# Causal mask of the row maxima moved from TensorE's matmuls into one fused VectorE instruction, with the stage's loops written out

## The chip, the cores and the metric

The kernel runs on one core of a Trainium2 chip. TensorE, VectorE, ScalarE and GpSimd work beside each other and meet at semaphores; SyncE issues the DMAs. The metric is the device time of one launch in microseconds: 903.62 us as the median of three runs (902.7 to 904.41). The times of the profile come from one further execution.

## The reference

Four layers run one after another over an input of 8 batches x 512 tokens x 128 features: dilated attention with a ternary feed-forward, a gated attention, a causal attention with grouped heads, and a mixture of experts. The change concerns the third:

```python
q = (x @ wq.T).reshape(B, S, 16, 8)
k = (x @ wk.T).reshape(B, S, 4, 8)      # repeated for 16 heads
v = (x @ wv.T).reshape(B, S, 4, 8)
attn = jnp.einsum('bqhd,bkhd->bhqk', q, k) / sqrt(8)
attn = jnp.where(causal, attn, -inf)
attn = jax.nn.softmax(attn, axis=-1)
out = jnp.einsum('bhqk,bkhd->bqhd', attn, v)
```

B is 8, S is 512, with 16 heads. A softmax is computed with the maximum of each row taken off first, so every head needs the 512 maxima of its causal rows.

## The kernel before, in words

The causal attention is a stage of its own (`causal_attention_phase`, names beginning with `d_`). The stage ahead of it (`projection_phase`, names `c_`) computes the queries and keys, splits each into bf16 parts that add up to the fp32 value, and SyncE stores them in DRAM (`q_stack`, `k_stack`) by batch. Its end waits for all these stores, and then for all engines. The causal stage loads the stacks back as 96 rows (`Qs`, `Ks`), one pair of buffers for even and one for odd batches.

A batch is worked on twice. In the *first* pass (function `first` on TensorE, `maxima` on VectorE) TensorE multiplies queries with keys, tokens of the query along the partitions, into two PSUM banks `pS` that alternate. A head has three *fills* of a bank: 512 keys for the last 128 queries (f = 0), 384 keys (f = 1), and 256 + 128 keys for the first two blocks of queries (f = 2). Behind each product a second matmul of an identity with a 128x128 triangle of -1e30 (`top.mask_bf`) adds the causal mask to its last 128 columns. VectorE reduces each block to a maximum per row (`mx`). A fill starts when VectorE is through with the fill two before it (semaphore `S_max`), and VectorE starts on a fill when TensorE has ended it (semaphore `S`). When a batch has all its maxima, `split` cuts them into three bf16 parts, TensorE turns them (`rows`), and a trip through DRAM makes them six more rows beside the stacks.

In the *second* pass (`second`) TensorE multiplies keys with queries, this time with the maxima taken off, into `pT`; ScalarE takes the exponential into `P`; GpSimd zeroes the triangle there (`affine_select`, L1167); TensorE multiplies with the values (`values`, into `pO`); ScalarE copies `pO` out, TensorE turns it (`by_token`, into `pM`), and VectorE divides by the sums (`divide`).

The order is written out by hand. A step (one batch) has 8 pairs of heads of 3 units. TensorE does in a unit: the second pass for this unit, two fills of the first pass of a later batch, and, by a pattern of period six units (`turn`), one of four value products, or the turning of an output, or neither. VectorE does the same two fills' maxima and, once in six units, a `divide`. The fills run three pairs (`LEAD`) ahead of the batch: the last three pairs of step n fill heads of batch n + 2. Ahead of the first step, all of batch 0 and six heads of batch 1 are filled with nothing beside them.

Step 0 and step 7 are written out; steps 1 to 6 are a hardware loop of three rounds of two steps (`Fori` in `steps`), so waits in it compare with counts held in registers. Since each round is the same code, step 6 too loads and fills a batch n + 2 = 8, which does not exist: `q_stack` and `k_stack` have a ninth entry, into which the projection stage stores the last batch a second time (`(0, 1, 1)` in its SyncE block), and the first pass of six heads is run on it. Nobody uses these maxima.

Of the kernel before, what the change touches and what calls it, by code (L numbers as in the profile page):

```python
# [35 lines left out]


def wait_alone(eng, sem, count, unit=1):


    if not isinstance(count, int):
        count = eng.to_reg(count)
        eng.wait_ge(sem, unit)
    eng.wait_ge(sem, count)
# [749 lines left out]
def projection_phase(nc, top, dram):  # L794

    with ExitStack() as ctx:
# [217 lines left out]
def causal_attention_phase(nc, top, dram):  # L1014
# [11 lines left out]
    with ExitStack() as ctx:  # L1026
        ph = Phase(nc, ctx, "d_")
        sm = ph.sems("zeros ones ones_from max_ones S S_max part1 rest1 part2 rest2 parts mT_psum mT ST P masked PV O_sb O_T rden O_tok")
# [15 lines left out]
        rden = ph.sb("rden", [128, QT, 2, 2])  # L1044
        pS = [ph.ps(f"pS{k}", [128, 512]) for k in two]
# [11 lines left out]
        def wait(eng, sem, value):  # L1057

            if not isinstance(value, int) or value > 0:
                eng.wait_ge(sem, value)  # L1060

        def steps(eng, step):
# [15 lines left out]

        def turn(pair, unit, at):
# [5 lines left out]
        def turns(n, pair, unit, at):  # L1085

            got = turn(pair, unit, at)
            ended = isinstance(n, int) and n == B
            if got is None or (got[0] == 0 and ended) or (got[0] == 1 and isinstance(n, int) and n == 0):
                return []  # L1090
# [5 lines left out]
        parity = [0]  # L1096

        def par(n):

            if isinstance(n, int):  # L1100
                parity[0] = n % 2
            else:
                parity[0] = 1 - parity[0]
            return parity[0]

        with nc.Block() as block:

            @block.sync
            def _(sp):
# [22 lines left out]
                def step(n, m, more):  # L1132
                    c = par(n)
                    if more:
# [3 lines left out]
                        if not (isinstance(n, int) and n + 2 > B):  # L1138
# [4 lines left out]
                        sp.wait_ge(sm["ST"], n * NT + NT)  # L1143
                        load_stack(n + 2, c, 1)
# [7 lines left out]
                steps(sp, step)  # L1152

                for a in two:
                    sp.wait_ge(stacks[0][a], 64 * (B // 2 + 1))

            @block.gpsimd
            def _(pool):
                def step(n, m, more):
                    par(n)  # L1160
                    for pair in range(HEADS // 2):
                        for unit in range(3):

                            wait_alone(pool, sm["P"], n * NT + 3 * pair + unit + 1)
# [22 lines left out]
                steps(pool, step)  # L1187

            @block.vector
            def _(dve):  # L1190
                def maxima(n, c, some):
                    for k, f in some:
                        h, fill = ORDER[k], 3 * k + f
                        dve.wait_ge(sm["S"], n * NS + fill + 1)
                        src = pS[fill % 2]
                        if f < 2:
                            last = nc.vector.reduce_max(mx[c][:, 3 - f, h:h + 1], src[:, 0:512 - 128 * f], AX.X)  # L1197
                        else:
                            nc.vector.reduce_max(mx[c][:, 1, h:h + 1], src[:, 0:256], AX.X)  # L1199
                            last = nc.vector.reduce_max(mx[c][:, 0, h:h + 1], src[:, 256:384], AX.X)  # L1200
# [32 lines left out]
                def step(n, m, more):  # L1233
                    c = par(n)
                    for pair in range(HEADS // 2):
                        if more and pair == SPLIT_AT:
                            split(n + 1, 1 - c)
                        for unit in range(3):
                            if more:
                                for ahead, k, f in fills(pair)[2 * unit:2 * unit + 2]:  # L1240
# [8 lines left out]
                steps(dve, step)  # L1249
# [5 lines left out]
            def _(act):  # L1255
# [11 lines left out]
                def step(n, m, more):  # L1267
                    c = par(n)
# [16 lines left out]
                steps(act, step)  # L1285
# [5 lines left out]
            def _(pe):  # L1291
# [3 lines left out]
                def first(n, m, c, some):  # L1295

                    for k, f in some:
# [60 lines left out]
                def rows(n, c):  # L1358

                    if not (isinstance(n, int) and n == 0):  # L1360
                        wait_alone(pe, sm["O_tok"], (n - 1) * NG + 1)
                    wait_alone(pe, sm["parts"], n + 1)
# [5 lines left out]
                def step(n, m, more):  # L1368
                    c = par(n)
                    for pair in range(HEADS // 2):  # L1370
                        for unit in range(3):
                            second(n, m, c, pair, unit)
                            if more:
                                for ahead, k, f in fills(pair)[2 * unit:2 * unit + 2]:
# [8 lines left out]
                steps(pe, step)  # L1383
# [410 lines left out]
```

## Time and profile before

| | |
|---|---|
| launch, median of 3 runs | 903.62 us |
| span of the profiled execution | 900.7 us (no time of its own is given beyond the span; the median stands 2.9 us above it) |
| TensorE busy | 643.0 us (71%) |
| VectorE busy | 559.2 us (62%) |
| ScalarE busy | 403.3 us (45%) |
| GpSimd busy | 222.6 us (25%) |
| maxima L1197, L1199, L1200 | 160.9 + 56.3 + 37.6 us in 268 + 134 + 134 instructions |
| mask matmuls | 111.4 us in 536 instructions |
| GpSimd's triangle in `P`, L1167 | 101.0 us in 256 instructions |
| the page's first group of products of the first pass, all four shapes | 150.4 us in 536 instructions |

The causal stage runs from its first loads at 402 us to 754 us. A busy time sums what the records cover; matmuls overlap one another, so TensorE's is more than it needs. What one instruction costs its engine is the distance from its start to the next start where neither waits. "Idle before" names whom an engine waited for.

### The profile page before, as it was taken

Reading aid. Unit: us, or ns where it says so; the run is one execution under the profiler, and the core shown is the slowest. Engines: PE = TensorE matmul, PEld = TensorE weight load, DVE = VectorE, ACT = ScalarE, POOL = GpSimd, SP = SyncE. Lnnn points to the kernel's source line nnn. Section 1 sums busy time; section 2 is a strip of 40 time slices with the busy share of each in tenths; the row PEclk is TensorE's granted clock in tenths of the full one; section 3 lists DMA queues with packets and bytes.
Section 4 is the critical chain, followed back from the end, with each engine's and each line's share of the span. In section 5 each row is a group of like instructions: output and inputs, shape, how many; then the busy total and the mean of one; then the engine's idle time right before and its main releaser. Section 6 shows DMA issues by size and latency. Waiting matters only on the chain. (4 is left out here: it accounts for less than half of the span.)

```text
span 900.7 us, 13426 instructions
## 1 busy us (share of the span) xinstructions
PE 643.0 (71%) x4232; PEld 372.4 (41%) x4232; DVE 559.2 (62%) x1764; ACT 403.3 (45%) x794; POOL 222.6 (25%) x340
## 2 busy tenths in 40 slices
PE   0816338938754480708899999999999996789651
PEld 0816328117644270403244445454444523555320
DVE  5786974042463535307878878788787801478897
ACT  3682565410203424400046566665665673456541
POOL 1040310010003032333023333333333341134344
PEclk9957655555965665755579999999999997799896
DMA  6000000000000050253001111111011100000001
GB/s 236 1 0 1 1 1 1 0 2 1 1 1 0 1 175 0 70 168 81 17 1 49 36 37 30 33 40 42 26 38 33 36 13 1 0 1 1 23 24 47
DMA packets 19369, 28.61 MB, mean 32 GB/s; under 512 B 3310, under 2 KB 15102, under 8 KB 19146
## 3 DMA queue, kind: packets, MB, share of 16 engines
q1 hardware_dynamic: 18746, 25.94, 9.5%
q10 hardware_dynamic: 576, 2.10, 0.6%
q8 instruction: 23, 0.38, 0.2%
q14 instruction: 24, 0.20, 0.1%
HBM read 14.57 MB, written 11.35 MB: 29 GB/s over the span
## 5 line engine op out<-in xcount | busy, mean ns | idle before, releaser
L1276 ACT ACTIVATE d_P<-d_pT 128x768 f32<-128x768 f32 (+1 forms) x192 | 167.9, 881 | 110.8 <-PE d_pT L1293 110.8
L1197 DVE TENSOR_REDUCE d_mx<-d_pS 128x1 f32<-128x512 f32 (+1 forms) x268 | 160.9, 620 | 66.2 <-PE d_pS L1293 61.5
L1293 PE MATMUL d_pS<-d_Ks,d_Qs 96*128 96x512 bf16 (+3 forms) x536 | 150.4, 329 | 31.2 <-DMA d_Ks<-k_stack 25.1
L1167 POOL TENSOR_SCALAR_AFFINE_SELECT d_P<-d_P 128x256 f32<-128x256 f32 x256 | 101.0, 406 | 233.5 <-ACT d_P L1276 233.4
L1293 PE MATMUL d_pS<-mask_bf,ident_bf 128*128 128x128 bf16 x536 | 111.4, 236 | 0.0
L1293 PE MATMUL d_pT<-d_Qs,d_Ks 102*128 102x512 bf16 (+3 forms) x512 | 103.7, 305 | 1.1 <-ACT d_P L1276 0.5
L1293 PE MATMUL d_pO<-d_P,d_V 128*32 128x512 f32 (+3 forms) x1024 | 96.5, 451 | 1.9 <-POOL d_P L1167 1.5
L1293 PEld LDWEIGHTS d_pS<-d_Ks,d_Qs 96*128 96x128 bf16 x536 | 54.2, 101 | 100.1 <-DVE d_mx L1197 32.8
L1623 PE MATMUL e_PE<-gate_expT,e_oT 128*128 128x512 f32 x128 | 62.5, 634 | 11.0 <-DVE e_T L1519 10.4
L421 PE MATMUL a_PS<-ident,N 128*128 128x128 f32 x96 | 21.5, 403 | 63.5 <-ACT N L320 51.6
L1199 DVE TENSOR_REDUCE d_mx<-d_pS 128x1 f32<-128x256 f32 x134 | 56.3, 420 | 13.5 <-PE d_pS L1293 11.1
L1293 PEld LDWEIGHTS d_pT<-d_Qs,d_Ks 102*128 102x128 bf16 x512 | 35.7, 99 | 69.1 <-ACT d_P L1276 49.5
L1450 POOL TENSOR_TENSOR e_T<-e_T 128x512 f32<-128x512 f32 x32 | 40.7, 1279 | 93.5 <-DVE e_T L1519 77.9
L1293 PEld LDWEIGHTS d_pS<-mask_bf,ident_bf 128*128 128x128 bf16 x536 | 55.5, 104 | 7.1 <-issue 0.3
L1605 ACT ACTIVATE e_T<-e_PE,e_comb 128x128 f32<-128x128 f32 x128 | 34.7, 383 | 45.0 <-PE e_PE L1623 19.6
L421 PEld LDWEIGHTS a_PS<-ident,N 128*128 128x128 f32 x96 | 17.8, 212 | 66.7 <-ACT N L320 54.6
L415 POOL TENSOR_TENSOR X<-X,a_nT 128x1024 f32<-128x1024 f32 x8 | 19.5, 2433 | 92.0 <-ACT a_nT L320 92.0
L1623 PEld LDWEIGHTS e_PE<-gate_expT,e_oT 128*128 128x128 f32 x128 | 24.7, 205 | 40.8 <-issue 23.3
L990 PE MATMUL c_PA<-ident,c_a 128*128 128x128 f32 x32 | 7.9, 428 | 46.6 <-ACT c_a L950 46.6
L320 ACT ACTIVATE N<-X,a_nb,a_rs 128x128 f32<-128x128 f32 x96 | 37.8, 479 | 1.1 <-DVE a_nb L161 0.8
L1200 DVE TENSOR_REDUCE d_mx<-d_pS 128x1 f32<-128x128 f32 x134 | 37.6, 281 | 0.0
L1258 ACT ACTIVATE d_mT<-d_pM 48x512 bf16<-48x512 bf16 x8 | 4.7, 590 | 65.3 <-PE d_pM L1364 65.2
(256 smaller groups left out, 1056.8 us busy)
## 6 DMA issues: line engine op xcount, KB each, us to landing
d_Qs<-q_stack SPq DMA_DIRECT2D x36, 192.0 KB, 2.9
q_stack<-c_Qp SPq DMA_DIRECT2D x9, 384.0 KB, 2.7
q_stack<-c_Qp SPq DMA_DIRECT2D x9, 256.0 KB, 3.0
X<-in_x_dram ACTq DMA_DIRECT2D x4, 512.0 KB, 7.7
d_V<-V SPq DMA_DIRECT2D x8, 256.0 KB, 2.3
out_dram<-e_moe SPq DMA_DIRECT2D x4, 512.0 KB, 2.6
d_Ks<-k_stack SPq DMA_DIRECT2D x36, 48.0 KB, 2.8
w_qkvT<-in_w_qkvT_dram SPq DMA_DIRECT2D x1, 1536.0 KB
```

What stands on the lines that cost most here:

```text
L320: last = nc.scalar.activation(dst(t), src(t), ACT.Identity, bias=nb[c][:, t:t + 1], scale=rs[c][:, t:t + 1])
L415: nc.gpsimd.tensor_tensor(X[c][:, :, :], X[c][:, :, :], y[c][:, :, :], ALU.add).then_inc(sm[s + "_x"], 1)
L421: last = nc.tensor.transpose(dst(t), src(t), ident)
L1167: last = nc.gpsimd.affine_select(out=view, in_=view, compare_op=ALU.is_ge, fill=0.0, base=0, pattern=[[0, 2], [1, 128]], channel_multiplie ...
L1197: last = nc.vector.reduce_max(mx[c][:, 3 - f, h:h + 1], src[:, 0:512 - 128 * f], AX.X)
L1199: nc.vector.reduce_max(mx[c][:, 1, h:h + 1], src[:, 0:256], AX.X)
L1200: last = nc.vector.reduce_max(mx[c][:, 0, h:h + 1], src[:, 256:384], AX.X)
L1276: nc.scalar.activation(P[pair % 4][:, :, P_AT[unit]:P_AT[unit] + w], pT[(3 * pair + unit) % 2][:, :, 0:w], ACT.Exp, scale=float(HD4) ** -0 ...
L1293: return nc.tensor.matmul(out, lhsT, rhs, start=start, stop=stop)
L1450: nc.gpsimd.tensor_tensor(T[u % 4][:, 0:NE // 2, :], T[u % 4][:, 0:NE // 2, :], T[u % 4][:, NE // 2:NE, :], ALU.add).then_inc(sm["halved"], 1)
L1605: last = nc.scalar.activation(T[u % 4][:, e, :], PE_[1][:, e, :], ACT.Copy, scale=comb[u // CT][:, u % CT, e:e + 1])
L1623: return nc.tensor.matmul(out_, lhsT, rhs, start=start, stop=stop)
```

## The change

VectorE's `tensor_tensor_reduce` takes the product from PSUM and a mask from SBUF, adds them, writes the sum (bf16, to `masked_S`, read by nobody) and gives the maximum of each row. The mask `wide_mask` is 384 columns of zero and then the triangle; each block reads its last w columns, and it is built once by a memset and a copy with one wait. The mask matmuls go. The loop is replaced by eight written-out steps, so all waits compare with constants (`wait_alone` goes), and nothing is stored, loaded or filled for a ninth batch (`fills_of`, `n + 2 < B`).

```diff
-                    for b in (0, 1, 1) if k == CHUNKS - 1 else (0, 1):
-                        entry = 2 * k + b + (1 if n_stored[c] == 12 * (k // 2) + 12 else 0)
+                    for b in two:
+                        entry = 2 * k + b
...
+        wide_mask = ph.sb("wide_mask", [128, 512], BF16)
+        masked_S = [ph.sb(f"masked_S{k}", [128, 512], BF16) for k in two]
...
-            step(0, 0, True)
-            with eng.Fori(0, B // 2 - 1) as i:
-                step(2 * i + 1, i, True)
-                step(2 * i + 2, i + 1, True)
-            step(B - 1, B // 2 - 1, False)
+            for n in range(B):
+                step(n, n // 2, n % 2, n < B - 1)
...
+        def fills_of(n, pair, unit):
+
+            return [(ahead, k, f) for ahead, k, f in fills(pair)[2 * unit:2 * unit + 2] if n + ahead < B]
...
-                        sp.wait_ge(sm["ST"], n * NT + NT)
-                        load_stack(n + 2, c, 1)
+                        if n + 2 < B:
+                            sp.wait_ge(sm["ST"], n * NT + NT)
+                            load_stack(n + 2, c, 1)
...
-                        if f < 2:
-                            last = nc.vector.reduce_max(mx[c][:, 3 - f, h:h + 1], src[:, 0:512 - 128 * f], AX.X)
-                        else:
-                            nc.vector.reduce_max(mx[c][:, 1, h:h + 1], src[:, 0:256], AX.X)
-                            last = nc.vector.reduce_max(mx[c][:, 0, h:h + 1], src[:, 256:384], AX.X)
+                        for q, at in ((3, 0),) if f == 0 else ((2, 0),) if f == 1 else ((1, 0), (0, 256)):
+                            w = 128 * q + 128
+                            last = nc.vector.tensor_tensor_reduce(
+                                out=out_[:, at:at + w], in0=src[:, at:at + w], in1=wide_mask[:, 512 - w:512],
+                                scale=1.0, scalar=LOWEST, op0=ALU.add, op1=ALU.max,
+                                accum_out=mx[c][:, q, h:h + 1])
...
+                nc.vector.memset(wide_mask[:, 0:384], 0.0)
+                nc.vector.tensor_copy(wide_mask[:, 384:512], top.mask_bf[:, :]).then_inc(sm["mask_wide"], 1)
+                dve.wait_ge(sm["mask_wide"], 1)
...
-                            mm(dst[:, at:at + w], Qs[c][0:ALL_ROWS, i, 128 * q:128 * q + 128],
-                               Ks[c][0:ALL_ROWS, h // 4, 0:w], True, False)
-                            last = mm(dst[:, at + w - 128:at + w], top.ident_bf[:, :], top.mask_bf[:, :],
-                                      False, True)
+                            last = mm(dst[:, at:at + w], Qs[c][0:ALL_ROWS, i, 128 * q:128 * q + 128],
+                                      Ks[c][0:ALL_ROWS, h // 4, 0:w])
```

On TensorE, in step 0 behind the turning of the maxima of batch 0, one unit and the start of the next stand like this before (`d_pT` is the second pass, `d_pS` a fill):

```order
L1293 MATMUL d_pT<-d_Qs,d_Ks 128x384 x2
L1293 MATMUL d_pS<-d_Ks,d_Qs 128x256
L1293 MATMUL d_pS<-mask_bf,ident_bf 128x128
L1293 MATMUL d_pS<-d_Ks,d_Qs 128x128
L1293 MATMUL d_pS<-mask_bf,ident_bf 128x128
L1293 MATMUL d_pS<-d_Ks,d_Qs 128x512
L1293 MATMUL d_pS<-mask_bf,ident_bf 128x128
L1293 MATMUL d_pT<-d_Qs,d_Ks 128x256
```

The same place in the changed kernel:

```order
L1274 MATMUL d_pT<-d_Qs,d_Ks 128x384 x2
L1274 MATMUL d_pS<-d_Ks,d_Qs 128x256
L1274 MATMUL d_pS<-d_Ks,d_Qs 128x128
L1274 MATMUL d_pS<-d_Ks,d_Qs 128x512
L1274 MATMUL d_pT<-d_Qs,d_Ks 128x256
```

Four matmuls a head go, each behind its product; nothing else is in another place.

On VectorE, at the first head of the stage (before, L1197 twice, for f = 0 and f = 1) and what follows it:

```order
L1197 TENSOR_REDUCE d_mx<-d_pS 128x1 x2
L1199 TENSOR_REDUCE d_mx<-d_pS 128x1
L1200 TENSOR_REDUCE d_mx<-d_pS 128x1
```

And now, from the building of the mask on:

```order
L1225 MEMSET d_wide_mask 128x192
L1226 COPY d_wide_mask<-mask_bf 128x128
L1177 ISA d_masked_S,d_mx<-d_pS,d_wide_mask 128x512
L1177 ISA d_mx 128x1
L1177 ISA d_masked_S,d_mx<-d_pS,d_wide_mask 128x384
L1177 ISA d_mx 128x1
L1177 ISA d_masked_S,d_mx<-d_pS,d_wide_mask 128x256
L1177 ISA d_mx 128x1
L1177 ISA d_masked_S,d_mx<-d_pS,d_wide_mask 128x128
L1177 ISA d_mx 128x1
```

Each of the four reductions of a head has become two instructions: the fused one and one that writes the row's maximum out of the engine's accumulator.

On SyncE, at the end of the projection stage, before (the last six are the second copy of the last batch):

```order
L832 DMA q_stack<-c_Qp 128x3x512
L834 DMA k_stack<-c_Kp 32x3x512
L832 DMA q_stack<-c_Qp 128x2x512
L834 DMA k_stack<-c_Kp 32x2x512
L832 DMA q_stack<-c_Qp 128x512
L834 DMA k_stack<-c_Kp 32x512
L819 UNCONDITIONAL_BRANCH
L1108 UNCONDITIONAL_BRANCH
L1114 DMA d_Qs<-q_stack 48x2048
```

And now, where these rows are the only copy:

```order
L823 DMA q_stack<-c_Qp 128x3x512
L825 DMA k_stack<-c_Kp 32x3x512
L823 DMA q_stack<-c_Qp 128x2x512
L825 DMA k_stack<-c_Kp 32x2x512
L823 DMA q_stack<-c_Qp 128x512
L825 DMA k_stack<-c_Kp 32x512
L810 UNCONDITIONAL_BRANCH
L1091 UNCONDITIONAL_BRANCH
L1097 DMA d_Qs<-q_stack 48x2048
```

The branch and the first load of the causal stage have moved up by six DMAs.

## Rows read from the trace of the kernel before

**Rows 1.** The page, part 2: granted TensorE clock in 40 slices of 22.5 us

```profile
PEclk9957655555965665755579999999999997799896
```

**Rows 2.** Timeline, TensorE, one period: start us, us, engine, line, operation, tiles

```profile
541.05 0.49 PE L1293 MATMUL d_pT<-d_Qs,d_Ks 102*128 102x384 bf16 x2
...
543.03 0.50 PE L1293 MATMUL d_pT<-d_Qs,d_Ks 102*128 102x256 bf16 x4
...
543.54 0.22 PE L1293 MATMUL d_pS<-mask_bf,ident_bf 128*128 128x128 bf16 x1
...
543.60 0.27 PE L1293 MATMUL d_pS<-d_Ks,d_Qs 96*128 96x256 bf16 x1
...
544.76 0.61 PE L1293 MATMUL d_pT<-d_Qs,d_Ks 102*128 102x512 bf16 x2
...
546.37 0.50 PE L1293 MATMUL d_pT<-d_Qs,d_Ks 102*128 102x384 bf16 x2
...
547.72 0.50 PE L1293 MATMUL d_pT<-d_Qs,d_Ks 102*128 102x256 bf16 x4
...
548.76 0.59 PE L1293 MATMUL d_pT<-d_Qs,d_Ks 102*128 102x512 bf16 x2
...
550.32 0.49 PE L1293 MATMUL d_pT<-d_Qs,d_Ks 102*128 102x384 bf16 x2
```

**Rows 3.** Timeline, VectorE, where it does not wait

```profile
540.40 1.16 DVE L1197 TENSOR_REDUCE d_mx<-d_pS 128x1 f32<-128x512 f32 x2
...
541.48 0.25 DVE L1222 RECIPROCAL d_rden<-d_pM 128x16 f32<-128x16 f32 x1
...
542.14 0.41 DVE L1199 TENSOR_REDUCE d_mx<-d_pS 128x1 f32<-128x256 f32 x1
```

**Rows 4.** Groups of VectorE (a two-part instruction), then timeline of ScalarE's accumulator reads

```profile
L1480 DVE MATCH_VALUE_LOAD e_index<-e_best,e_logit 128x8 f32 x32 | 2.3, 73 | 0.0
...
762.91 0.19 ACT L1581 ACTIVATION_READ_ACCUMULATOR e_moe<-e_h 128x1 f32 x1
763.00 0.29 ACT L1581 ACTIVATE e_moe<-e_h 128x128 f32<-128x128 f32 x1
```

**Rows 5.** Timeline of the experts stage, VectorE beside GpSimd

```profile
807.82 1.27 POOL L1450 TENSOR_TENSOR e_T<-e_T 128x512 f32<-128x512 f32 x1 [3.62 <-DVE e_T L1519]
808.60 1.22 DVE L1460 TENSOR_TENSOR e_h<-e_PA,N 128x1024 f32<-128x1024 f32 x1
...
831.74 2.34 POOL L1445 TENSOR_TENSOR e_moe<-e_h,X 128x1024 f32<-128x1024 f32 x1
831.84 2.26 DVE L1501 TENSOR_TENSOR e_w<-e_w 128x8 f32<-128x8 f32 x1
```

**Rows 6.** Timeline, SyncE's last stores and TensorE's first fill

```profile
390.88 0.44 SPq L832 DMA_DIRECT2D q_stack<-c_Qp  x1
...
393.76 0.44 SPq L834 DMA_DIRECT2D k_stack<-c_Kp  x1
...
406.78 0.61 PE L1293 MATMUL d_pS<-d_Ks,d_Qs 96*128 96x512 bf16 x1 [25.09 <-DMA d_Ks<-k_stack]
```

**Rows 7.** Timeline, TensorE in the last step, which has no fills

```profile
720.30 1.07 PE L1293 MATMUL d_pO<-d_P,d_V 128*32 128x512 f32 x8
...
727.10 1.06 PE L1293 MATMUL d_pO<-d_P,d_V 128*32 128x512 f32 x8 [0.38 <-issue]
```

**Rows 8.** Timeline, ScalarE, the same instruction of three steps

```profile
519.68 0.59 ACT L1258 ACTIVATE d_mT<-d_pM 48x512 bf16<-48x512 bf16 x1
...
557.28 0.59 ACT L1258 ACTIVATE d_mT<-d_pM 48x512 bf16<-48x512 bf16 x1 [0.31 <-PE d_pM L1364]
...
595.26 0.59 ACT L1258 ACTIVATE d_mT<-d_pM 48x512 bf16<-48x512 bf16 x1 [0.30 <-PE d_pM L1364]
```

**Rows 9.** Timeline, VectorE ahead of the first step, heads 1 and 16 of batch 0

```profile
409.03 0.42 DVE L1199 TENSOR_REDUCE d_mx<-d_pS 128x1 f32<-128x256 f32 x1 [0.34 <-PE d_pS L1293]
...
440.49 0.42 DVE L1199 TENSOR_REDUCE d_mx<-d_pS 128x1 f32<-128x256 f32 x1
```

More of the change, by code:

```diff
@@ L35 @@
 NEG = -8.0
[L38 to L44, printed above, removed]
 class Phase:
@@ L1027, in causal_attention_phase @@
         ph = Phase(nc, ctx, "d_")
-        sm = ph.sems("zeros ones ones_from max_ones S S_max part1 rest1 part2 rest2 parts mT_psum mT ST P masked PV O_sb O_T rden O_tok")
+        sm = ph.sems("mask_wide zeros ones ones_from max_ones S S_max part1 rest1 part2 rest2 parts mT_psum mT ST P masked PV O_sb O_T rden O_tok")
         two = range(2)
@@ L1057, in wait, with steps @@
         def wait(eng, sem, value):
-            if not isinstance(value, int) or value > 0:
+            if value > 0:
                 eng.wait_ge(sem, value)
-        def steps(eng, step):
-            step(0, 0, True)
-            with eng.Fori(0, B // 2 - 1) as i:
-                step(2 * i + 1, i, True)
-                step(2 * i + 2, i + 1, True)
-            step(B - 1, B // 2 - 1, False)
+        def steps(step):
+            for n in range(B):
+                step(n, n // 2, n % 2, n < B - 1)
         def fills(pair):
@@ L1087, in turns @@
             got = turn(pair, unit, at)
-            ended = isinstance(n, int) and n == B
-            if got is None or (got[0] == 0 and ended) or (got[0] == 1 and isinstance(n, int) and n == 0):
+            if got is None or (got[0] == 0 and n == B) or (got[0] == 1 and n == 0):
                 return []
@@ L1130, in max_rows, with step @@
                             .then_inc(rows_in[c], 16)
-                def step(n, m, more):
-                    c = par(n)
+                def step(n, m, c, more):
                     if more:
@@ L1151, in _, with step @@
                 max_rows(0, 0, 0)
-                steps(sp, step)
-                for a in two:
-                    sp.wait_ge(stacks[0][a], 64 * (B // 2 + 1))
+                steps(step)
             @block.gpsimd
             def _(pool):
-                def step(n, m, more):
-                    par(n)
+                def step(n, m, c, more):
                     for pair in range(HEADS // 2):
                         for unit in range(3):
-                            wait_alone(pool, sm["P"], n * NT + 3 * pair + unit + 1)
+                            pool.wait_ge(sm["P"], n * NT + 3 * pair + unit + 1)
                             for at in ((P_AT[0],), (P_AT[1],), P_AT[2:])[unit]:
@@ L1186, in _ @@
                             .then_inc(sm["max_ones"], 1)
-                steps(pool, step)
+                steps(step)
             @block.vector
@@ L1231, in divide, with step @@
                     last.then_inc(sm["O_tok"], 1)
-                def step(n, m, more):
-                    c = par(n)
+                def step(n, m, c, more):
                     for pair in range(HEADS // 2):
@@ L1239, in step @@
                             if more:
-                                for ahead, k, f in fills(pair)[2 * unit:2 * unit + 2]:
+                                for ahead, k, f in fills_of(n, pair, unit):
                                     b, _, b_c = others(n, m, c, ahead)
@@ L1248, in _ @@
                 maxima(1, 1, everything[:6 * LEAD])
-                steps(dve, step)
+                steps(step)
                 for pair, unit in LAST_TURNS:
@@ L1284, in _ @@
                 rows(0, 0)
-                steps(act, step)
+                steps(step)
                 for pair, unit in LAST_TURNS:
@@ L1358, in rows @@
                 def rows(n, c):
-                    if not (isinstance(n, int) and n == 0):
-                        wait_alone(pe, sm["O_tok"], (n - 1) * NG + 1)
-                    wait_alone(pe, sm["parts"], n + 1)
+                    wait(pe, sm["O_tok"], (n - 1) * NG + 1)
+                    pe.wait_ge(sm["parts"], n + 1)
                     for q in range(QT):
@@ L1366, in rows, with step @@
                     last.then_inc(sm["mT_psum"], 1)
[L1368 to L1369 removed]
+                def step(n, m, c, more):
                     for pair in range(HEADS // 2):
@@ L1373, in step @@
                             if more:
-                                for ahead, k, f in fills(pair)[2 * unit:2 * unit + 2]:
+                                for ahead, k, f in fills_of(n, pair, unit):
                                     first(*others(n, m, c, ahead), [(k, f)])
@@ L1382, in _ @@
                 first(1, 0, 1, everything[:6 * LEAD])
-                steps(pe, step)
+                steps(step)
                 for pair, unit in LAST_TURNS:
```

18 lines of the change are left out of this document (5 added, 13 removed).

## The prediction, made before the changed kernel had run

> **What bounds the kernel now.** I read the shares of the engines first: TensorE 71%, VectorE 62%, so neither is idle enough to be ignored nor full enough to be the bound alone. The chain of waits begins only at 754 us, behind the causal stage, because all engines meet there. So the stage is in series with the rest, and what it saves the kernel saves. The change touches this stage and the end of the one before it. TensorE's clock is at its low level (1.2 GHz) in slices 18 and 19, ahead of the first step, and at its high level (2.4 GHz) from slice 21 to 32, which takes in steps 1 to 6 and the first part of step 7 [rows 1].
>
> Then the timeline of one period, which is two pairs or four heads. Its six units start on TensorE at 541.05, 543.03, 544.76, 546.37, 547.72 and 548.76, and the next period at 550.32 [rows 2]: 1.98, 1.73, 1.61, 1.35, 1.04 and 1.56 us, 9.27 in all. The first four hold the value products and are long; the fifth holds none, the sixth the turning of an output.
>
> VectorE's price of a maximum is its start-to-start distance where it does not wait. A 512 and a 384 block took from 540.40 to 541.48, 1.08 us [rows 3]. A reduction of 256 columns is recorded with 0.41 us and an addition of 1024 with 1.22 [rows 3, 5]: 0.81 us for 768 columns, 1.04 to 1.06 ns each, and I take 1.042. The 896 columns are then 0.933 of the 1.08 us, so an instruction costs its columns + 0.073 us. The three fills of a head cost 0.606 (f = 0), 0.473 (f = 1) and 0.267 + 0.133 + 0.146 = 0.546 us. A divide takes from 541.48 to 542.14, 0.66 us [rows 3]. By unit, with the fills in their order (1, 1.15; 2, 1.02; 3, 1.08; 4, 1.15; 5, 1.02; 6, 1.08 + 0.66 = 1.74), VectorE needs 7.16 us in a period.
>
> The two banks let one engine run ahead by about a unit at most. I therefore take, for each unit, the longer of the two engines: 1.98, 1.73, 1.61, 1.35, 1.04, 1.74, sum 9.45. The trace has 9.27, so this rule is 2% too long, and I use it for differences only.
>
> **The change part by part.**
>
> *The stores.* The second copy of the last batch is issued from 390.88 to 393.76 + 0.44 = 394.20 us, 3.3 us, and nothing computes there: TensorE's first fill waited 25.09 us for a DMA [rows 6]. The causal stage begins when the stores have landed, so the whole 3.3 us goes: **-3.3**. It could be 2.8 to 3.8, since a store's landing and not its issue ends the wait.
>
> *Six heads of no use.* Step 6's last three pairs lose their fills. A period without fills is 727.10 - 720.30 = 6.80 us [rows 7] against 9.27, so three pairs save 1.5 x 2.47 = **-3.7**. The turning of batch 7's maxima in that step could come 0.5 us late for want of cover.
>
> *The loop.* From 519.68 to 557.28 both steps are of one round, 37.60 us; from 557.28 to 595.26 a round ends between them, 37.98 us [rows 8]. So a round's end costs 0.38 us, and there are an entry, two returns and an exit: between 0.8 (returns alone) and 1.5 us, **-1.0**. What the waits on registers cost is not seen apart; in the first units TensorE's matmuls stand close behind one another, so I take 0, and a gain from them would come on top.
>
> *Mask matmuls.* From 543.54 to 543.60 one is worth 0.06 us of TensorE at the high clock [rows 2]. 16 of them leave a period: 3, 3, 2, 3, 3, 2 by unit. TensorE's units become 1.80, 1.55, 1.49, 1.17, 0.86, 1.44.
>
> *The fused instruction.* It reads a product in PSUM and bf16 in SBUF. The nearest row is an addition of such a pair over 1024 columns, 1.22 us [rows 5], that is 1.067 for the columns and 0.15 that its neighbours partly cover; the reductions have the same 0.15. So I take the main part at the price of the reduction it replaces.
>
> *The accumulator read,* a second instruction with each, 16 in a period. The trace has none on VectorE. From below: the load half of a two-part instruction is recorded with 73 ns, and costs somewhat less from start to start, so 0.055 us. From above: ScalarE's accumulator read is recorded with 0.19 us [rows 4], if the engine may do nothing beside it; but on ScalarE the next instruction started 0.09 us after the read (762.91 to 763.00) [rows 4]. I take 0.073 us, what any small instruction costs here beyond its columns, and keep 0.055 and 0.19. VectorE's units become 1.15 + 0.22, 1.02 + 0.22, 1.08 + 0.15, 1.15 + 0.22, 1.02 + 0.22, 1.74 + 0.15 = 1.37, 1.24, 1.23, 1.37, 1.24, 1.89. The longer of the two: 1.80, 1.55, 1.49, 1.37, 1.24, 1.89, sum 9.34. Against 9.45 that is -0.11 a period. 106 heads are filled inside steps, 26.5 periods: **-2.9**. What the units with value products win, the others give back. Each further 10 ns of a read costs 0.08 a period (8 of the 16 reads lie in units that VectorE sets), 2.1 us in all.
>
> *The edge of a batch.* A step of 37.60 us is four periods of 9.27 and 0.52 for the split and the turning of the maxima. With VectorE later than before, less of the split is covered; I add the same again for six steps, rounded down: **+2.5** (0 to 4).
>
> *Ahead of the first step.* Head 1 to head 16 took 440.49 - 409.03 = 31.46 us, 2.10 a head [rows 9], where VectorE alone needs 1.63. The rest is the round trip of a bank at the low clock. The read lengthens that trip by what the missing mask matmul (0.11 us at this clock) shortens it: **0**, for 22 heads. Building the wide mask lies in the 25 us in which VectorE waits for the stacks. Loads of batch 8 that go were beside other work.
>
> Sum: -3.3 - 3.7 - 1.0 - 2.9 + 2.5 = -8.4 us, from the profiled span 900.7 to 892.3. The median stands 2.9 us above that span, so **895.2 us**.
>
> One rule of the skill speaks to the read. The microarchitecture page (Trainium skill, "Vector Engine (DVE) Microarchitecture Reference", section 5.2, Measured stream behaviour on trn2) gives 1.0417 ns a column and about 75 ns an instruction after overlap, the same for programs of several micro-ops. Taken for the read this is an estimate of 0.076 us, and the sum would stand within 1 us of the one above; no row here shows it for an accumulator.
>
> **The rivals.**
>
> *The accumulator read is not overlapped (slower).* If VectorE is held until the main part has ended and the read has been written, a read costs 0.19 us. VectorE's units become 1.72, 1.59, 1.46, 1.72, 1.59, 2.12, the longer ones 1.80, 1.59, 1.49, 1.72, 1.59, 2.12 = 10.31, +0.86 a period, +22.8 us; ahead of the first step a head takes 1.63 + 0.76 = 2.39 instead of 2.10, +6.4 us. With -8.0 for stores, heads and loop and +4 for the edges: +25, **929 us**. It tips at a read of about 0.105 us. For it: no row has this instruction, and its value goes to the engine's buffer release, as S_max now hangs on it. Against: ScalarE's pair overlaps.
>
> *VectorE and GpSimd block each other (slower).* The maxima now read SBUF, and GpSimd works a third of the period (256 instructions of 0.4 us in 32 periods: 3.2 us in each). An instruction of 8 columns took 2.26 us beside GpSimd's of 2.34, both of its inputs in SBUF [rows 5]. If a fused maximum that starts in such a time waits a quarter of a us, a third of 16 gives +1.3 a period on VectorE, 0.7 after overlap: +18, **914 us**. Against: an addition with one input in PSUM took 1.22 us though GpSimd's instruction covered its first 0.5 us [rows 5].
>
> This is what the Trainium skill says ("SBUF — State Buffer", Who interferes with whom): two SBUF inputs contend with GpSimd's reads, one does not. By that rule the rival costs nothing here, and the trace agrees with 1.22 against 2.26 us.
>
> *The reads are nearly free (faster).* At 0.03 to 0.055 us a read, with the split covered: -2.9 - 5 and no +2.5, **888 us**. The rows of a loading half with 73 ns speak for it a little.
>
> *TensorE's clock falls.* Its stage loses 16 short matmuls a period, but step 7 without any fill stays at the high level in slice 32 [rows 1]. In a step at 1.2 GHz a period would be some 4 us longer; 26.5 of them, 1000 us. I give it 2%.
>
> **How the numbers follow.** Forecast (read 0.06 to 0.09 us) 0.60: 890 to 901. Nearly free reads 0.12. A read of 0.09 to 0.12, with which the gain vanishes, 0.11: 900 to 907. Not overlapped 0.10; blocked by GpSimd 0.05; clock 0.02. A measurement of this kernel tells 0.2%, 1.8 us, from no change. Faster takes the forecast, the free reads and a little of the third, 0.74; same 0.07; slower the rest, 0.19. Leaving out most of the last three and the lowest tail, the range is 885 to 912.
>
> **What would show it.** The fused instruction's mean at 512 columns should be 0.69 us and the next start 0.61 + 0.07 later; a period from 541 on, read at the second pass's 512-column unit, 9.1 to 9.2 us; the stage's first fill 3.3 us earlier, near 403.5; no fills after pair 4 of step 6, and 3.7 us less there; VectorE busy near 90% in the steps, its waits for `d_pS` shrunk and TensorE's waits for `d_mx` grown. I am wrong if the read's start-to-start is over 0.1 us, if the fused part has a second cycle a column, or if TensorE's clock drops between 460 and 740 us.

## The result, and the profile after

The changed kernel took 875.68 us (median of 4, 875.22 to 875.80) against 903.16 (4 runs, 896.22 to 904.41): ratio 0.970, with a 95% interval of 0.966 to 0.974. The forecast was 895.2, range 885 to 912. The direction was right, the gain was 27.5 us instead of 8.4. The profiled execution took 875.76 us and spans 874.0 us (the one before spans 900.7).

Of several versions single executions (of e6 and e11 two each) reach the causal stage 12 to 15 us earlier than the others, so below stages are compared by their length (first fill of the causal stage to first matmul `e_PA` of the next) beside the medians.

The page of the kernel after, parts 1 and 2 (busy us, share, instructions; granted clock in 40 slices of 21.9 us):

```profile
PE 611.4 (70%) x3672; PEld 336.9 (39%) x3672; DVE 553.2 (63%) x2254; ACT 402.2 (46%) x794; POOL 222.5 (25%) x340
...
PEclk9967655555966575565569999999999996899896
```

TensorE lost 31.6 us of work. VectorE's busy time is no larger (559.2 before), though it executes 490 more instructions (512 reads came, 24 reductions of the ninth batch went): the reads' records lie beside others. The clock stays high through the steps, as before [rows 1], and in both kernels it falls for 3.4 us in the last value products, which the account below needs.

Groups of VectorE after, shapes apart, from 370 us on (count, busy us, mean ns, idle before them):

```profile
L1177 DVE CUSTOM_DVE_ANT_0 d_masked_S<-d_pS,d_wide_mask 128x512 bf16<-128x512 f32 x128 | 88.2, 689 | 22.3 <-PE d_pS L1274 22.2
L1177 DVE CUSTOM_DVE_ANT_0 d_masked_S<-d_pS,d_wide_mask 128x384 bf16<-128x384 f32 x128 | 71.1, 555 | 14.2 <-PE d_pS L1274 13.5
L1177 DVE CUSTOM_DVE_ANT_0 d_masked_S<-d_pS,d_wide_mask 128x256 bf16<-128x256 f32 x128 | 53.9, 421 | 5.2 <-PE d_pS L1274 2.4
L1177 DVE DVE_READ_ACCUMULATOR2_ANT d_mx<- 128x1 f32 x512 | 42.5, 83 | 0.0
L1177 DVE CUSTOM_DVE_ANT_0 d_masked_S<-d_pS,d_wide_mask 128x128 bf16<-128x128 f32 x128 | 36.6, 286 | 0.0
```

The fused instruction's 689 ns at 512 columns are the forecast's 0.69. Its means would be far above this if GpSimd held it up. So the main part was priced rightly; what of the read's 83 ns? The timeline of VectorE (start, us):

```profile
527.12 0.08 DVE L1177 DVE_READ_ACCUMULATOR2_ANT d_mx<- 128x1 f32 x1
527.12 0.42 DVE L1177 CUSTOM_DVE_ANT_0 d_masked_S<-d_pS,d_wide_mask 128x256 bf16<-128x256 f32 x1
527.47 0.08 DVE L1177 DVE_READ_ACCUMULATOR2_ANT d_mx<- 128x1 f32 x1
527.47 0.28 DVE L1177 CUSTOM_DVE_ANT_0 d_masked_S<-d_pS,d_wide_mask 128x128 bf16<-128x128 f32 x1
...
527.69 0.69 DVE L1177 CUSTOM_DVE_ANT_0 d_masked_S<-d_pS,d_wide_mask 128x512 bf16<-128x512 f32 x1
528.31 0.08 DVE L1177 DVE_READ_ACCUMULATOR2_ANT d_mx<- 128x1 f32 x1
528.31 0.55 DVE L1177 CUSTOM_DVE_ANT_0 d_masked_S<-d_pS,d_wide_mask 128x384 bf16<-128x384 f32 x1
528.79 0.08 DVE L1177 DVE_READ_ACCUMULATOR2_ANT d_mx<- 128x1 f32 x1
```

A fused instruction and its read start 0.62 us apart for 512 columns (527.69 to 528.31) and 0.48 for 384, which is the price of the plain reduction in the forecast (0.606 and 0.473) plus 0.01. The next fused instruction starts within 0.01 us of the read. The read lies in the last 0.08 us of the long record ahead of it, in which the next long one starts too. Over five batches (second to seventh `d_mT`), where nothing waits between, the median distance from one long instruction to the next is 0.616, 0.483, 0.345 and 0.212 us for 512, 384, 256 and 128 columns; for the plain reductions of e1 (below) it is 0.608, 0.475, 0.332 and 0.198. So the fused instruction and its read together cost VectorE 0.008 to 0.014 us more than the reduction, where the forecast had 0.073.

TensorE over one period, which answers to [rows 2]:

```profile
526.84 0.60 PE L1274 MATMUL d_pT<-d_Qs,d_Ks 102*128 102x512 bf16 x2
...
527.82 0.34 PE L1274 MATMUL d_pS<-d_Ks,d_Qs 96*128 96x384 bf16 x1 [0.17 <-DVE d_mx L1177]
...
528.43 0.49 PE L1274 MATMUL d_pT<-d_Qs,d_Ks 102*128 102x384 bf16 x2
...
530.25 0.50 PE L1274 MATMUL d_pT<-d_Qs,d_Ks 102*128 102x256 bf16 x4
...
531.79 0.60 PE L1274 MATMUL d_pT<-d_Qs,d_Ks 102*128 102x512 bf16 x2
...
533.28 0.50 PE L1274 MATMUL d_pT<-d_Qs,d_Ks 102*128 102x384 bf16 x2
...
534.57 0.34 PE L1274 MATMUL d_pT<-d_Qs,d_Ks 102*128 102x256 bf16 x2
```

The units from 526.84 on are 1.59, 1.82, 1.54, 1.49 and 1.29 us, and the one before (525.93) 0.91: 8.64. From one turned output to the one a period later (517.43, 526.07, 534.70 on ScalarE) it is 8.63, against 9.27 before and 9.1 to 9.2 expected.

ScalarE's instruction of [rows 8], after:

```profile
508.42 0.59 ACT L1240 ACTIVATE d_mT<-d_pM 48x512 bf16<-48x512 bf16 x1 [0.22 <-PE d_pM L1342]
...
543.76 0.59 ACT L1240 ACTIVATE d_mT<-d_pM 48x512 bf16<-48x512 bf16 x1 [0.50 <-PE d_pM L1342]
...
579.10 0.59 ACT L1240 ACTIVATE d_mT<-d_pM 48x512 bf16<-48x512 bf16 x1 [0.50 <-PE d_pM L1342]
```

A batch is 35.34 us, the same each time, where it was 37.60 and 37.98 in turn. (Here and below a batch is the distance of two such instructions, which turn out the maxima of a batch.) SyncE's last store and TensorE's first fill and first matmul of the next stage, for [rows 6]:

```profile
390.33 0.43 SPq L825 DMA_DIRECT2D k_stack<-c_Kp  x1
...
403.40 0.93 PE L1274 MATMUL d_pS<-d_Ks,d_Qs 96*128 96x512 bf16 x2 [21.03 <-DMA d_Ks<-k_stack]
...
727.62 1.94 PE L1607 MATMUL e_PA<-ident,O 128*128 128x128 f32 x8 [1.61 <-PEq L57]
```

The first of this last row of stores (24, before 30) began at 377.10 us (before 376.43). The first fill comes 3.4 us earlier than before, as forecast. The stage lasts 324.22 us; before it was 347.57 (406.78 to 754.35). From there to the end both kernels take 146.4 us.

The waits over nearly six batches (470 to 680 us; us in total, times, longest):

```profile
ACT d_P L1257 <- PE d_pT L1274: 64.3, 95, 1.0
PEld d_pS L1274 <- DVE d_mx L1177: 34.2, 96, 0.6
...
DVE d_masked_S L1177 <- PE d_pS L1274: 24.4, 62, 0.6
```

Both engines wait for each other, by turns, over the two banks. Over the matching stretch of before (481 to 707 us) VectorE had waited for `d_pS` 29.3 + 6.6 us and TensorE's loads for VectorE 14.2 + 7.6. VectorE's busy share over five batches went from 81 to 87%, where near 90 was expected; TensorE's from 99 to 97%.

### The profile page after: what moved, and what is told of

Same layout as the page of the kernel before. It is cut to its first block and busy times, and to the rows that moved or that the text cites. A ratio compares the mean times of both kernels' runs of the same rounds, so it can differ in the third digit from the quotient of the medians.

```text
span 874.0 us, 11330 instructions
## 1 busy us (share of the span) xinstructions
PE 611.4 (70%) x3672; PEld 336.9 (39%) x3672; DVE 553.2 (63%) x2254; ACT 402.2 (46%) x794; POOL 222.5 (25%) x340
## 5 line engine op out<-in xcount | busy, mean ns | idle before, releaser
L1177 DVE CUSTOM_DVE_ANT_0 d_masked_S<-d_pS,d_wide_mask 128x512 bf16<-128x512 f32 (+3 forms) x512 | 224.5, 488 | 41.7 <-PE d_pS L1274 38.2
L1274 PE MATMUL d_pS<-d_Ks,d_Qs 96*128 96x512 bf16 (+3 forms) x512 | 132.5, 332 | 36.0 <-DMA d_Ks<-k_stack 21.0
L1274 PEld LDWEIGHTS d_pS<-d_Ks,d_Qs 96*128 96x128 bf16 x512 | 45.7, 99 | 112.1 <-DVE d_mx L1177 74.3
L1582 ACT ACTIVATE e_T<-e_PE,e_comb 128x128 f32<-128x128 f32 x128 | 34.7, 383 | 45.1 <-PE e_PE L1600 19.7
L1177 DVE DVE_READ_ACCUMULATOR2_ANT d_mx<- 128x1 f32 x512 | 42.5, 83 | 0.0
L1274 PEld LDWEIGHTS d_pO<-d_P,d_V 128*32 128x32 f32 x1024 | 20.9, 109 | 36.3 <-issue 28.6
L1202 DVE RECIPROCAL d_rden<-d_pM 128x16 f32<-128x16 f32 x32 | 8.1, 254 | 38.9 <-PE d_pM L1333 38.9
L1501 DVE TENSOR_REDUCE e_moe<-e_T 128x128 f32<-128x512 f32 x32 | 32.4, 1035 | 0.1
```

What stands on the lines that cost most here:

```text
L1177: last = nc.vector.tensor_tensor_reduce(out=out_[:, at:at + w], in0=src[:, at:at + w], in1=wide_mask[:, 512 - w:512], scale=1.0, scalar=LO ...
L1274: return nc.tensor.matmul(out, lhsT, rhs, start=start, stop=stop)
L1501: nc.vector.tensor_reduce(moe[u // CT][:, u % CT, :], T[u % 4][:, 0:NE // 2, :].rearrange("p e d -> p d e"), AX.X, ALU.add).then_inc(sm["s ...
L1582: last = nc.scalar.activation(T[u % 4][:, e, :], PE_[1][:, e, :], ACT.Copy, scale=comb[u // CT][:, u % CT, e:e + 1])
```

## The experiments

The theories: **M** (the read costs nothing from start to start; the gain is TensorE's mask matmuls, the heads and the stores), **R** (the read or the fused instruction costs about what the forecast gave it, and a larger gain elsewhere hides it), **U** (the hardware loop and its waits on registers were the large cost), **V** (TensorE's wait for a bank is one of order within the unit). Letters that one text alone uses are told there.

| kernel | median (runs) | batch | period | stage |
|---|---|---|---|---|
| before | 903.16 (4) | 37.60 / 37.98 | 9.27 | 347.57 |
| e1: loops written out, old mask, old maxima | 891.69 (4) | 37.54 | 9.27 | 341.21 |
| e3: e1 with the fused instruction | 897.24 (4) | 37.77 | 9.32 | 343.09 |
| e2: e1 without mask matmuls | 872.25 (4) | 35.13 | 8.57 | 321.55 |
| after | 875.68 (4) | 35.34 | 8.63 | 324.22 |
| e4: after, memset of 1 column behind each read | 876.31 (4) | 35.51 | 8.67 | 324.93 |
| e5: after, memset of 64 columns there | 887.01 (4) | 36.35 | 8.88 | 336.29 |
| e8: after, stores of the last batch twice | 880.09 (4) | 35.34 | 8.63 | 324.18 |
| e6: after, TensorE's unit interleaved | 868.97 (6) | 34.67 | 8.45 | 318.07 |
| e7: e6 with e2 | 870.35 (6) | 34.57 | 8.43 | 317.77 |
| e9: after again | 875.77 (6) | 35.34 | 8.63 | 325.25 |
| e10: e6 again | 870.59 (6) | 34.67 | 8.45 | 319.50 |
| e11: e1, interleaved | 886.10 (4) | 37.86 | 9.30 | 342.43 |

Batch, period and stage are read from the profiled execution of each, the first two as above. Ratios to the kernel before in their own session: e5 0.983 [0.978, 0.987], e8 0.977 [0.972, 0.982], e6 0.959 [0.953, 0.964], e7 0.964 [0.961, 0.966], e9 0.969 [0.961, 0.977], e10 0.967 [0.962, 0.972], e11 0.987 [0.978, 0.996]. For e1 to e4 none is on record; their medians stand beside 902.69 us of the kernel before. With 2% as the line, e6, e7, e9 and e10 are faster than the kernel before, and e5, e8 and e11 are unclear.

**e1, e2, e3: one part at a time.** e1 is the changed kernel with both old parts back:

```diff
-                            last = nc.vector.tensor_tensor_reduce(... op0=ALU.add, op1=ALU.max, ...)
+                        if f < 2:
+                            last = nc.vector.reduce_max(mx[c][:, 3 - f, h:h + 1], src[:, 0:512 - 128 * f], AX.X)
...
-                            last = mm(dst[:, at:at + w], Qs..., Ks...)
+                            mm(dst[:, at:at + w], Qs..., Ks..., True, False)
+                            last = mm(dst[:, at + w - 128:at + w], top.ident_bf[:, :], top.mask_bf[:, :], False, True)
```

> The changed kernel with the old mask: the mask matmuls are back and VectorE reduces the masked product; loops written out and no ninth batch. Theory M (the gain beyond the ninth batch and the loop ends comes from the mask matmuls that left, because the accumulator read costs nothing): stores 4.1, six heads 3.7 and loop ends 1.0 us stay, so 903.2 - 8.8 = 894 us, period 9.27 us. Rival U (waits on constants instead of registers speed up every unit): most of the gain stays, 880 us or less, and the period is under 9.0 us.

e2 takes the first hunk alone, and so leaves the mask out of the maxima; e3 the second alone, and so adds the mask twice.

> The changed kernel with plain reductions over the unmasked product, neither mask matmuls nor fused instruction: the maxima are then taken over later keys as well, so this leaves out the causal mask of the maxima. Theory M (the fused instruction and its read cost together what the reduction costs): 875.7 us within 1.5, period 8.64 us. Rival R (each read costs 0.055 us or more from start to start): at least 12 us faster, 863 us, and a period near 8.2 us.

> The changed kernel with the mask matmuls added back, fused instruction kept, so the mask is added twice. Theory M: as e1, 894 us and a period of 9.27 us, since the fused instruction costs what the reduction does. Rival R (read at 0.055 to 0.073 us): 12 us or more above e1, 906 us, period 9.7 us.

The same instruction of ScalarE in e1, and then in e2:

```profile
553.58 0.59 ACT L1239 ACTIVATE d_mT<-d_pM 48x512 bf16<-48x512 bf16 x1 [0.24 <-PE d_pM L1343]
...
591.11 0.59 ACT L1239 ACTIVATE d_mT<-d_pM 48x512 bf16<-48x512 bf16 x1 [0.24 <-PE d_pM L1343]
```

```profile
496.60 0.59 ACT L1239 ACTIVATE d_mT<-d_pM 48x512 bf16<-48x512 bf16 x1 [0.49 <-PE d_pM L1341]
...
531.73 0.59 ACT L1239 ACTIVATE d_mT<-d_pM 48x512 bf16<-48x512 bf16 x1 [0.49 <-PE d_pM L1341]
```

e1's period is before's, 9.27: waits on registers cost nothing that shows, and U falls. The stage is 6.4 us shorter: 4.7 for the heads and the ends of rounds, and 1.65 for the clock near its end. The last value products of the stage, in before, e1 and after:

```profile
747.34 4.01 PE L1293 MATMUL d_pO<-d_P,d_V 128*32 128x512 f32 x32 [0.88 <-POOL d_P L1167]
```

```profile
739.31 2.36 PE L1273 MATMUL d_pO<-d_P,d_V 128*32 128x512 f32 x32 [0.89 <-POOL d_P L1146]
```

```profile
720.58 4.05 PE L1274 MATMUL d_pO<-d_P,d_V 128*32 128x512 f32 x32 [0.88 <-POOL d_P L1146]
```

The granted clock was at its low level there in before (747.3 to 750.7 us) and after (720.7 to 724.1), and high in e1. Such a fall is in the traces of before, after, e5 and e8 and in no other of the table; it adds 1.65 to 1.7 us to their stages and says nothing of the change. From e1 to e2 the matmuls alone go: -19.7 us, R falls. From e2 to after the fused instruction and its read come in place of the plain reduction: a batch 35.13 to 35.34, 0.21 us for 64 pairs, so 3 ns of time for each (the whole stage gives 2.7 us, of which 1.7 are the clock at its end). Where TensorE has its matmuls (e1 to e3) they cost as little, +1.9. The median of e3 lies 3 us over M's 894 because its first fill came 2.9 us late.

**e4, e5: what a small instruction costs.** A memset behind each fused instruction and its read, of one column (e4) or of 64 (e5):

```diff
+                            last = nc.vector.memset(pad[fill % 2][:, at // 256:at // 256 + 1], 0.0)
```

> The changed kernel with one more small VectorE instruction (a memset of one column) behind each accumulator read, and the bank's release after it: 16 more a period, each at 0.07 us or a little more. If only the price of the read was wrong in the prediction and its rule of the longer engine by unit is right, this is the kernel that was priced: period 8.64 + 0.58 = 9.2 us, +15.4 us in the steps, +4 us ahead of them, +1 at the edges of the batches: 896 us (892 to 900). If the rule is wrong and VectorE has slack in the units, under 885 us.

> The changed kernel with a memset of 64 columns behind each accumulator read, 16 more a period. In e4 a memset of one column took no time from start to start; 64 columns must hold the engine for at least their 0.067 us. Theory V (the prediction's rule was right and only the read was priced too high): at 0.067 to 0.075 us each this is the kernel that the prediction priced: period 8.63 + 0.5 to 0.6 = 9.1 to 9.2 us, 13 to 16 us in the steps and 4 ahead of them, 893 to 896 us. Rival S (VectorE has slack in the steps, TensorE alone sets them): period under 8.8 us and under 883 us.

VectorE in e4, and then in e5:

```profile
526.77 0.42 DVE L1178 CUSTOM_DVE_ANT_0 d_masked_S<-d_pS,d_wide_mask 128x256 bf16<-128x256 f32 x1
527.12 0.08 DVE L1178 DVE_READ_ACCUMULATOR2_ANT d_mx<- 128x1 f32 x1
527.13 0.28 DVE L1178 CUSTOM_DVE_ANT_0 d_masked_S<-d_pS,d_wide_mask 128x128 bf16<-128x128 f32 x1
527.15 0.06 DVE L1182 MEMSET d_pad<- 128x1 f32 x1
527.34 0.08 DVE L1178 DVE_READ_ACCUMULATOR2_ANT d_mx<- 128x1 f32 x1
527.35 0.69 DVE L1178 CUSTOM_DVE_ANT_0 d_masked_S<-d_pS,d_wide_mask 128x512 bf16<-128x512 f32 x1
```

```profile
526.50 0.11 DVE L1182 MEMSET d_pad<- 128x64 f32 x1
526.53 0.67 DVE L1178 CUSTOM_DVE_ANT_0 d_masked_S<-d_pS,d_wide_mask 128x512 bf16<-128x512 f32 x1
527.12 0.08 DVE L1178 DVE_READ_ACCUMULATOR2_ANT d_mx<- 128x1 f32 x1
527.17 0.11 DVE L1182 MEMSET d_pad<- 128x64 f32 x1
527.20 0.49 DVE L1178 CUSTOM_DVE_ANT_0 d_masked_S<-d_pS,d_wide_mask 128x384 bf16<-128x384 f32 x1
```

Both expectations missed high, and the misses say most. (Under 885 us is what e4's text gives for a wrong rule of the longer engine; but its memset turned out to cost VectorE almost nothing, so e4 does not test the rule. e5 ended between its two theories.)

In e4 the long instructions start at 526.77, 527.13 and 527.35, 0.36 and 0.22 us apart with two small ones between; after, without the memset, the same three start at 527.12, 527.47 and 527.69, 0.35 and 0.22 apart. By the medians over five batches a memset puts the next long instruction off by 5 to 9 ns. A batch grew by 0.17 us for 64 memsets, 3 ns of time each. So a one-column instruction behind a long one does not have a fee of 0.07 us of its own.

In e5 the distance from a 512-column instruction to the next long one is 0.67 us (526.53 to 527.20) instead of 0.62; over the four shapes the medians grew by 0.015 (128 columns) to 0.07 us (384), 0.05 on average. These 0.05 us, 16 times, are 0.8 us of VectorE in a period, and the period grew by 0.25, a batch by 1.0. (The stage's 12.1 us hold some 3 in which TensorE's clock stayed low longer: until 28 us after the first `d_mT`, and 18 in after.) So VectorE does bind in part: about a third of what it is given reaches the time, and the same third is in the reads (16 times 0.011 us, period +0.06 from e2 to after) and in e4 (16 times 0.007, +0.04). The forecast's rule would let half through, 8 of 16. The price of the read was what the forecast's loss hung on, and it was not there.

**e8: the stores alone.**

```diff
-                    for b in two:
+                    for b in (0, 1, 1) if k == CHUNKS - 1 else (0, 1):
```

> The changed kernel with the second store of the last batch back (six DMAs, 0.96 MB), nothing loaded from it. Theory M: the causal stage starts 4.1 us later and nothing else changes: 879.8 us. Rival H (the stores lie beside other work, and the earlier start came from elsewhere): 875.7 us.

From first store to first fill 29.80 us (376.40 to 406.20) against 26.30 after, +3.5; as this row of stores began 0.7 us earlier, the first fill came 2.8 us later. The stage is unchanged, the profiled execution 2.7 us and the median 4.4 us up. M's median (879.8) held; its 4.1 us were 2.8 to 3.5 in the trace.

**e6, e7, e10: the order within a unit.** TensorE puts one fill ahead of the value products and the other behind:

```diff
-                            if more:
-                                for ahead, k, f in fills_of(n, pair, unit):
-                                    first(*others(n, m, c, ahead), [(k, f)])
+                            some = fills_of(n, pair, unit) if more else []
+                            for ahead, k, f in some[:1]:
+                                first(*others(n, m, c, ahead), [(k, f)])
...
+                            for ahead, k, f in some[1:]:
+                                first(*others(n, m, c, ahead), [(k, f)])
```

The turning of the maxima (`rows`) moves behind the second fill with it. e7 leaves the mask out of the maxima as e2 does.

> The changed kernel with TensorE's order in a unit altered from second pass, fill, fill, value product to second pass, fill, value product, fill. Theory V (in the steps the two engines wait for each other in turn: VectorE starves while TensorE does the value product and makes TensorE wait in the short units): VectorE's waits for d_pS shrink, the period falls from 8.63 to about 8.4 us, 6 us in all, 870 us. Rival T (TensorE alone sets the period): no change, 875.7 within 1.5 us.

> As e6, with plain reductions over the unmasked product instead of the fused instruction; this leaves out the causal mask of the maxima. Theory V: e2's gain and e6's gain add, 872.3 - 6 = 866 us. Rival T: as e2, 872 us.

The waits of e6, 470 to 660 us:

```profile
PEld d_pS L1274 <- DVE d_mx L1177: 70.4, 152, 0.9
...
DVE d_masked_S L1177 <- PE d_pS L1274: 13.0, 49, 0.4
```

This stretch is 20 us shorter than the one of after above. Over five batches of each, VectorE's waits fell from 20.6 to 11.9 us and a batch by 0.67. The stage fell by 6.2, of which 4.5 lie between first and eighth `d_mT` and 1.7 are the clock at its end. TensorE's loads wait longer (64.5 against 28.5 us over the five), yet the period is shorter and TensorE's matmuls still cover 96% of it: most of those waits stand beside matmuls in flight. A batch of e7 is 0.10 us under e6's, where e2's was 0.21 under that of after: with this order the last nanoseconds matter less, and its expectation of 866 missed. The repetition, with the changed kernel on the same chip (the stage lengths in the two texts are 100 us too long; the traces of after and e6 have 324.22 and 318.07):

> The changed kernel again, as the measure beside which the two others stand. Theory M and its rivals alike: 875.7 us, period 8.63, causal stage 424.2 us from its first fill to the next stage's first matmul.

> The interleaved order again. Theory V (the second fill of a unit waited for the bank while the value products stood behind it): 869 to 870 us, the stage 418.1 us, period 8.45, 6 us under the changed kernel in the same session. Theory L (the 868.97 of the first time came from executions whose start was short, not from the stage): within 1 us of the changed kernel, though the stage of the one profiled execution was shorter.

870.59 against 875.77 us, stage 319.50 against 325.25, a batch 34.67 against 35.34: V holds and L falls. Of the 5.8 us of the stage the batches behind the first give 4.6 and the first 1.2, where the clock rose later in e9's trace than in e10's. It is the fastest full version, 5 to 7 us under the changed kernel by the medians and 4.5 in the steps.

**e11: the same order with the old mask.** The edit of e6 on e1.

> Mask by matmuls and plain reductions, loops written out, TensorE's units interleaved. Theory V: the wait between TensorE and VectorE was there before too, for the second of the two fills, so here too the order saves: before's period of 9.27 stands against a TensorE sum of 9.27 by definition of its units, of which its waits for maxima are a small part (14.2 us of loads in 8 steps waited, against 34.2 now), so less than half of the 6.1 us: 888 to 890 us against 891.7, period 9.15 to 9.22. Theory W (the order helps by what it does to the value products and not to the fills): 6 us here too, 885.6 us, period 9.09.

```profile
502.64 0.59 ACT L1239 ACTIVATE d_mT<-d_pM 48x512 bf16<-48x512 bf16 x1 [1.08 <-PE d_pM L1343]
...
540.50 0.59 ACT L1239 ACTIVATE d_mT<-d_pM 48x512 bf16<-48x512 bf16 x1 [1.08 <-PE d_pM L1343]
```

A batch of e11 on ScalarE is 37.86 us, 0.3 longer than e1's, and the stage 1.2 longer. Both theories missed; the median of 886.10 lies between two executions that reached the stage early (879.27 and 880.37; the profiled one had its first fill at 389.61 us, e1's at 403.44) and two that did not (891.83 and 893.49). VectorE's waits over five batches fell here too, from 31.5 to 23.0 us, and bought nothing. By the forecast's units TensorE with its mask matmuls is the longer engine in all but one, which fits. Without the mask matmuls the order gives 0.56 us a batch with plain reductions (e2 to e7) and 0.67 with fused ones; with them it costs 0.3. So the order pays only once TensorE is shorter.

## Why the prediction was wrong

By its own steps, in profiled us:

| step | forecast | measured |
|---|---|---|
| stores | -3.3 | -4.05 (first store to first fill 30.35 to 26.30); by e8 -3.5, by before to e1 -3.4 |
| six heads | -3.7 | -3.4 (before to e1, the clock at the end left out) |
| ends of rounds | -1.0 | -1.3 (before to e1) |
| ahead of the first step, up to the first `d_mT` | 0 | -3.1 (e1 to after) |
| mask matmuls, fused part, read; edge of a batch | -2.9 + 2.5 | -15.5 (e1 to after, first to eighth `d_mT`, 263.33 to 247.79) |
| clock at the stage's end | none | 0 (low for 3.4 us in before and in after) |
| start of the first store | 0 | +0.7 (376.43 to 377.10) |
| sum | -8.4 | -26.7, as the spans |

The medians differ by 27.5 us and the spans by 26.7, since the median stands 2.5 us above the profiled span before (903.16 and 900.7) and 1.7 after (875.68 and 874.0). From the eighth `d_mT` to the next stage after takes 43.5 us and e9, the same kernel without the fall of the clock, 41.8, as e1.

**The failed step is the price of the accumulator read.** The forecast took the 0.073 us that a long instruction costs beyond its columns for a fee of each instruction, and set 0.055 below it as the lowest. By the distances of starts the fused instruction and its read together cost 0.008 to 0.014 us more than the reduction (e1 to after), and e4's memset 0.005 to 0.009; of each 3 ns reached the time. So what the forecast took from the gain of the mask matmuls for the reads was not taken. The ScalarE rows [rows 4] had shown the pattern, a next start 0.09 us after a read of 0.19; it was used to bound the price from above and not to ask whether a read costs anything at all. The forecast's bound "somewhat less" than 73 ns had no row for a spacing.

**The rule that turned prices into a period was right for the matmuls.** With a read of 0, the longer engine by unit is 1.80, 1.55, 1.49, 1.17, 1.02 and 1.74, sum 8.77 against 9.45: -0.68 a period, and e1 to e2, where the matmuls alone go, measured -0.70. With 0.012 us for the read it is 8.85 and -0.60; measured -0.64 (9.27 to 8.63). 26.5 periods of it are -17, with the edges below -15.2, where the table has -15.5 (its row takes in six heads ahead of the first step). For what is added to VectorE the rule is too high: it gives 0.38 a period for e5's memsets, measured 0.25. The forecast's own rate (0.08 a period for each 10 ns) gives, for the missing 0.073, 0.57 us a period and 15 us in all; most of the error of 19 is this one number. The rival of nearly free reads, 888 us, stopped at 0.03 us, and so short of it.

**Ahead of the first step** 16 heads' starts now read, on VectorE:

```profile
405.46 0.42 DVE L1177 CUSTOM_DVE_ANT_0 d_masked_S<-d_pS,d_wide_mask 128x256 bf16<-128x256 f32 x1
...
434.02 0.43 DVE L1177 CUSTOM_DVE_ANT_0 d_masked_S<-d_pS,d_wide_mask 128x256 bf16<-128x256 f32 x1
```

28.56 us over 15 heads is 1.90 each, against 2.10 [rows 9]: the missing mask matmuls shorten the bank's round trip, and no read lengthens it. First fill to first `d_mT` went from 36.02 to 32.95; e1 has 36.09 and e2 32.60, so the matmuls alone did it. Forecast 0, measured -3: the second term that hung on the price of the read.

**The edge of a batch** is now 35.34 - 4 x 8.63 = 0.82 us, before 37.60 - 4 x 9.27 = 0.52: +0.3 a step, 1.8 in six, where +2.5 was set. Right in sign and nearly in size.

**Heads and rounds.** The rounds' ends, from the second to the seventh `d_mT`, were 188.98 us before and 187.67 in e1: -1.3 for -1.0. Of the rest of the 6.4, 1.65 us are the clock at the end and 3.4 the heads: 0.9 ahead of the eighth `d_mT` (37.60 to 36.69) and 2.5 from there to the last `d_pT` (36.57 to 34.09). That is the 3.7 of the forecast, near enough.

**The rivals.** Not overlapped: refuted by 0.00 us between read and next start. Blocked by GpSimd: refuted, each form's mean is within 5 ns of the reduction's in e1 (689, 555, 421 and 286 against 686, 554, 420 and 281). That is what the Trainium skill's rule ("SBUF — State Buffer", Who interferes with whom) gave for one input in SBUF, and the trace agrees. TensorE's clock did not fall in the steps.

The Trainium skill's figure beside the price ("Vector Engine (DVE) Microarchitecture Reference", section 5.2) had been about 75 ns an instruction after overlap. The runs agree for long ones (e1's 512 columns start 0.608 us apart, of which 0.533 are columns at its 1.0417 ns) and not for instructions of one column: 8 to 14 ns for a read with its fused part, 5 to 9 for e4's memset. The measurement decides.

## What to carry to other kernels

A fixed cost per instruction, fitted on long instructions, is no price for a tiny one behind them: before a forecast hangs on it, put its lower bound at zero, and look for any row in which a small instruction stands between two long ones, and at the distance between these. Price a change by the longer engine of each unit: 16 short matmuls of 0.06 us, that the forecast had hidden under VectorE, were worth 0.64 us of 9.27. Before a difference between two traces is put down to a change, compare the granted clock at the same place: a fall of 3.4 us in one of them was worth 1.65 us here. When one engine of a ping-pong has become shorter, try again orders that did nothing before: interleaving the fills was worth 0.67 us a batch after the change and cost 0.3 with the old mask.

## What was not expected of the hardware

- One-column instructions of VectorE (an accumulator read recorded with 83 ns, a memset with 59) start within some 0.03 us of the next long instruction. The read, together with the fused part, puts it off by 8 to 14 ns beyond a plain reduction, the memset (e4) by 5 to 9 more; the time grew by 3 ns for each.
- A memset of 64 columns, recorded with 112 ns, delays the next long one by 0.05 us on average (e5), and the long record behind it is shorter (657 against 689 ns at 512 columns), so neither record is a price: the distance of starts is.
- The fused add and maximum from PSUM and SBUF with a bf16 write costs what the plain reduction does within 0.014 us, its read included (records of 689 and 686 ns at 512 columns).
